# A memset of a scratch tile between GpSimd's row scatters in the 64-expert routing stages

## What is computed

```
x = x + 0.5 * _L0_ffn_ref(_layernorm(x), wg, shared_w1, shared_w2, expert_w1, expert_w2)
x = x + _L0_attn_ref(_layernorm(x), ...)
x = x + 0.5 * _L0_ffn_ref(_layernorm(x), ...)
...
```

## Time and profile before

| | us |
|---|---|
| median of 3 runs (3281.53 to 3283.92) | 3281.57 |
| span of the profiled execution | 3607.6 |
| TensorE busy in it | 2593.0 |
| VectorE busy | 2038.9 |
| GpSimd busy | 1846.4 |
| ScalarE busy | 1370.6 |
| scatters of line 1894, first routing stage, 160 | 159.7 |
| scatters of line 1894, second routing stage, 128 | 125.0 |

### The profile page before, as it was taken

How to read it: one execution, slowest core, us unless ns; L and a number is a source line. 1 busy time by engine, 2 the same in 40 slices (tenths; PEclk the granted TensorE clock), 3 DMA queues, 4 the chain that set the end, 5 groups by cost and what they waited for, 6 DMA issues and landing times. The chain is left out here.

```text
span 3607.6 us, 68811 instructions
## 1 busy us (share of the span) xinstructions
PE 2593.0 (72%) x24634; PEld 1681.5 (47%) x24634; DVE 2038.9 (57%) x5864; ACT 1370.6 (38%) x2937; POOL 1846.4 (51%) x2072
## 2 busy tenths in 40 slices
PE   1224994735499945689998899947388886999573
PEld 1113884423368834356555555536133332555362
DVE  4347334523443345547885587621699999787413
ACT  1111221301122222344665266622576763466323
POOL 5650775254317742126996213456488886123554
PEclk7666997856599977799999799978699999899786
DMA  9100896121019974331110101112221211111123
GB/s 373 48 1 8 213 224 155 45 66 31 27 41 226 226 191 108 138 120 21 19 19 3 20 19 30 48 55 56 102 94 48 94 62 40 22 20 35 43 80 92
DMA packets 222721, 294.13 MB, mean 82 GB/s; under 512 B 36704, under 2 KB 179583, under 8 KB 216288
## 3 DMA queue, kind: packets, MB, share of 16 engines
q1 hardware_dynamic: 172704, 249.85, 22.3%
q0 software_dynamic: 47616, 39.44, 5.8%
q10 hardware_dynamic: 2112, 1.05, 0.1%
HBM read 181.88 MB, written 107.12 MB: 80 GB/s over the span
## 5 line engine op out<-in xcount | busy, mean ns | idle before, releaser
L3783 POOL TENSOR_TENSOR l3am_db<-l3am_du,l3am_bs 128x1024 f32<-128x1024 f32 x127 | 298.0, 2367 | 39.9 <-DVE l3am_hh L4021 36.1
L4021 DVE TENSOR_TENSOR_SCAN l3am_hh<-l3am_dA,l3am_db 128x1024 f32<-128x1024 f32 x128 | 292.1, 2283 | 0.9 <-ACT l3am_dA L3921 0.7
L1217 POOL TENSOR_TENSOR l2a_pT<-l2a_pT,kept 128x512 int32<-128x512 int32 x213 | 265.1, 1280 | 45.4 <-ACT l2a_pT L1423 45.4
L3066 POOL DMA_INDIRECT l0f_table<-l0f2e_y,l0f2e_idx x128 | 178.9, 1398 | 177.1 <-DVE l0f2e_idx L3038 130.2
L3066 POOL DMA_INDIRECT l0f_table<-l0f1e_y,l0f1e_idx x128 | 179.6, 1403 | 139.2 <-DVE l0f1e_idx L3038 91.2
L4152 PE MATMUL l3am_y<-l3am_hc,ident 128*128 128x512 f32 x512 | 242.1, 596 | 0.0
L3921 ACT ACTIVATE l3am_dA<-l3am_dl,l3am_al 128x512 f32<-128x512 f32 x256 | 166.3, 682 | 130.8 <-DVE l3am_hh L4021 127.2
L1894 POOL DMA_INDIRECT l0f_rows<-l0f1r_row,l0f1r_idx x160 | 159.7, 998 | 103.1 <-issue 69.3
L1304 DVE CUSTOM_DVE_ANT_0 l2a_junk<-l2a_s,addend 128x256 f32<-128x256 f32 x486 | 178.1, 421 | 57.0 <-PE l2a_s L1540 44.6
L1297 DVE TENSOR_REDUCE l3f1a_mx<-l3f1a_s 128x2 f32<-128x512 f32 x243 | 156.5, 685 | 40.9 <-PE l3f1a_s L1540 32.4
L1297 DVE TENSOR_REDUCE l3f2a_mx<-l3f2a_s 128x2 f32<-128x512 f32 x243 | 156.4, 684 | 39.7 <-PE l3f2a_s L1540 32.1
(11 more groups left out here) (848 smaller groups left out, 7045.5 us busy)
## 6 DMA issues: line engine op xcount, KB each, us to landing
l3am_bs<-l3a_b SPq DMA_DIRECT2D x32, 1024.0 KB, 6.6
l0f1m_w<-in_L_ffn_expert_w SPq DMA_DIRECT2D x64, 384.0 KB
l0f2m_w<-in_L_ffn_expert_w SPq DMA_DIRECT2D x64, 384.0 KB
l1a_top<-l1a_kernel SPq DMA_DIRECT2D x16, 1024.0 KB, 12.6
l0f_rows<-blank SPq DMA_DIRECT2D x8, 1930.0 KB, 15.2
l0f1m_w<-in_L_ffn_expert_w SPq DMA_DIRECT2D x64, 192.0 KB
l0f2m_w<-in_L_ffn_expert_w SPq DMA_DIRECT2D x64, 192.0 KB
l3f_rows<-blank SPq DMA_DIRECT2D x8, 1440.0 KB, 11.6
```

What stands on the lines that cost most here:

```text
L1217: self.nc.gpsimd.tensor_tensor(t, t, self.kept[:, f // 8 % 2, :].unsqueeze(1).to_broadcast([P, 2, 2 * P]), ALU.mult).then_inc(self.cut_g, 1)
L3066: g.indirect_dma_start(out=tables[p], out_offset=bass.IndirectOffsetOnAxis(ap=idx[u % RING][:, a:a + 1], axis=0), in_=y[u % RING][:, a, :] ...
L3783: G.tensor_tensor(db[n % DB][:, :].rearrange("p (j t) -> p j t", j=CC), du[k % 2][:, :, :], bs[s // QUARTER][:, s % QUARTER, :].unsqueeze( ...
L4021: V.tensor_tensor_scan(hh[n % HH][:, :], dA[n % 2][:, :], db[n % DB][:, :], 0.0, ALU.mult, ALU.add).then_inc(h_ready, 1)
```

## The change

In `pool_scatter`, for the first three groups, GpSimd sets a tile of 128 x 384 numbers (`pause`) to zero before each scatter but the group's first. Each memset counts up a new semaphore (`paused`), and the next one waits for the count of the one before. That is 31 memsets per group, 93 per stage. The groups sent on a condition are left as they are. No other instruction reads the tile.

```diff
--- before.py
+++ after.py
@@ -1842,6 +1842,7 @@
     NONE = 65536.0
     SURE = -(-SLOTS // (K * GT))
     PER = 16 * TPG * K
+    PAUSE = 384
 
     def __init__(self, ph, c, m, front, logits, hidden, out, kept=GROUPS):
         E = self.E
@@ -1853,6 +1854,7 @@
         self.idx = [ph.sb(f"idx{i}", [P, TPG, self.K], U32) for i in range(self.DEPTH)]
         self.full = [ph.sb(f"full{i}", [P, 1], I32) for i in range(self.DEPTH)]
         self.least = ph.sb("leastf", [P, 1])
+        self.pause = ph.sb("pause", [P, self.PAUSE])
         self.base = ph.sb("base", [P, E])
         self.lg, self.gates, self.left, self.valid, self.key = (
             ph.sb(n, [P, TPG, E]) for n in ("lg", "gates", "left", "valid", "key"))
@@ -1874,6 +1876,7 @@
         self.h_done, self.silu_ready, self.gated, self.so_done, self.added = (
             ph.sem(s) for s in ("h_done", "silu_ready", "gated", "so_done", "added"))
         self.rows_free, self.sent = ph.sem("rows_free"), ph.sem("sent")
+        self.paused = ph.sem("paused")
         self.early = [ph.sem(f"early{i}") for i in range(2)]
         self.count = 0
 
@@ -1891,6 +1894,11 @@
         u = n % self.DEPTH
         for t in range(TPG):
             for j in range(self.K):
+                if (t or j) and n < self.SURE:
+                    k = n * (TPG * self.K - 1) + t * self.K + j - 1
+                    if k:
+                        g.wait_ge(self.paused, k)
+                    self.nc.gpsimd.memset(self.pause[:, :], 0.0).then_inc(self.paused, 1)
                 g.indirect_dma_start(out=self.m.rows, out_offset=bass.IndirectOffsetOnAxis(
                     ap=self.idx[u][:, t, j:j + 1], axis=0), in_=self.row[u][:, t, :], in_offset=None,
                     bounds_check=self.last_slot, oob_is_err=False).then_inc(sent, 16)
```

## The result

The changed kernel takes 3328.11 us (median of 4 runs, 3324.78 to 3330.27) against 3281.55 us before (3277.50 to 3283.92) in the same runs: a ratio of 1.014 with a 95% interval from 1.0125 to 1.0154, 46.6 us slower. The forecast was slower, 3348 us, in a range from 3283 to 3375.

What follows compares the result with a forecast made beforehand. The prediction took GpSimd's scatter sending to bound the first routing stage and nearly the second. 93 memsets per stage at 0.40 us cost 37 + 30 = 67 us on 3281.57, giving 3348 us, range 3283 to 3375.

Steps and rivals of the forecast that it cites:

- GpSimd's sending sets the stages' ends: Both routing stages: GpSimd's scatters end first stage by 9 us, fall 7 us short in second; 37 and 30 us paid.
- The memset's price: Each scatter with a memset: step 1.69 us against 1.28, so 0.40 us more, bounds 0.36 and 0.56.
- Memsets beside VectorE: Memsets writing while VectorE computes, both routing stages: bounded by nothing below and 8 us above, taken as nothing.
- Most of them exist only while every instruction and packet is recorded: Engine stalls while scatters are sent: said to come mostly with recording, their size matching the 326 us.
- The 326 us: Whole kernel: profiled span of 3607.6 us exceeds the plain median of 3281.57 us by 9.9%; charged to stalls under recording.
- The fall of the profiled span: Sign in the changed profile: span some 150 to 200 us shorter while plain runs get slower.
- The rebuilt undisturbed run: Plain run without stalls: first routing stage 108 us shorter than in the trace, second 169, later stages the other 49.
- Rival 1: Both routing stages: stalls are in plain runs too and pauses cure them, 194 us faster, 3088 us; chance 0.14.
- the prediction's cousin of rival 1: Behind scatters: late instruction blocks fetched by DMA stall plain runs too; 3088 us, little of rival 1's chance.

Runs made afterwards that it cites:

- e0: Kernel before, unchanged, profiled once more: 3279.94 us, ratio 1.0007, in a free batch (no engine held back).
- e1: Changed kernel with memsets in the first routing stage alone: 3312.01 us, ratio 1.0103 to the kernel before.
- e2: Changed kernel with memsets in the second routing stage alone: 3293.32 us, ratio 1.0047 to the kernel before.
- e3: Changed kernel with memsets of 128x16 instead of 128x384: 3280.64 us, ratio 1.0003 to the kernel before.
- e8: Changed kernel as it is, a second time: 3322.03 us against 3275.36 for the kernel before, ratio 1.0163.
- e4: Changed kernel with memsets of 128x192 instead of 128x384, held-back batch: 3513.94 us against 3607.50 for the kernel before, ratio 0.9719.
- e5: Changed kernel with memsets of 128x768 instead of 128x384, held-back batch: 3464.24 us against 3607.50 for the kernel before, ratio 0.9591.
- e7: Kernel before with the later groups' condition asked for each tile, 136 scatters for 160 in the first stage, held-back batch: 3584.12 us, ratio 0.9938.
- e9: Kernel before with later groups' condition asked per tile, plus memsets of 128x192 in the first stage, 128x384 in the second: 3298.43 us, ratio 1.0069.

## Why the prediction was right, and where it was not

**Slower because GpSimd's sending sets the stages' ends: shown.** e0's profile has GpSimd 20 us behind VectorE in the first stage (forecast 9) and 8 us ahead of it in the second (forecast 7). e1 makes the first stage 32 us longer with VectorE done at 235 us, e2 the second by 20 to 23, e3 neither.

**The memset's price: the term that was mis-sized.** The prediction took 0.98 + 0.13 + 0.42 + 0.16 = 1.69 us a step and 0.40 us a memset. The duration was 0.44 and the joint behind it 0.17, as taken, but the joint in front was 0.00 for 0.13: that row was a copy behind a scatter in another stage, and a memset starts at once. The price is 0.30 us, below the lower bound of 0.36. 93 x 0.30 = 28 us for 37 in each stage: 28 + 20 = 48 us for the 67 forecast, and 46.6 measured. This term makes 19 of the 20 us between 3348 and 3328.

**Memsets beside VectorE, bounded at 8 us and taken as nothing.** They lengthen VectorE's work by 14 us (2038.7 to 2052.9), 7 in each stage, more than the bound. That it cost nothing in the first stage is because GpSimd ends that stage by far: its end grew by 31 us, all of it GpSimd's sending. In the second stage what it may have cost is not told apart from the sending's 20 to 23 us.

**"Most of them exist only while every instruction and packet is recorded": the step that failed.** e0, e3 and e8 were recorded and have none of the stalls, and in the two held-back batches every timed run of the kernel before takes 3595 to 3638 us. The 326 us were the difference between a disturbed and an undisturbed batch, and I took the one variable that I could see, profiled or not, for the cause. The Trainium skill's page "NOTIFIC — the notification-queue block", section 7.1, was cited for a block that pushes back on its producers rather than lose a record. e0's trace bears out nothing of it for this kernel: as many instructions were recorded as in the first profile (68811), and no stall shows. The fall of the profiled span, named in advance as a sign (150 to 200 us, in fact 280), came, but from the batch.

**The rebuilt undisturbed run held all the same,** since it was worked out from rows and not from the cause. Forecast and e0: VectorE's side of the first stage 235 and 229 us, GpSimd's 244 and 252, what the stalls cost 108 and 100 us in the first stage, 169 and 165 in the second, 49 and 70 later. GpSimd's 8 us too few are mostly long scatters: e0's 160 took 163.8 us, 7 more than 160 x 0.98, and 12 of them over 1.2 us, of which the disturbed trace has 3. There was luck in it too: the runs of the result fell into a free batch, as the three before them had, and nothing in the prediction foresaw another kind.

**Rival 1 (the pauses cure the stalls, faster) is real where there are stalls.** Its mark, "1.28 us per scatter would be just too quick where 1.69 is not", holds for e4 in the first stage (1.43 us suffices) and for e5 in the second (1.90 us, not 1.43). It was priced against the wrong base: 194 us off 3281.57, where there is nothing to cure. From 3607 us it would be 3413. The widths beside the change's gave 3514 and 3464. Where a batch is held back the change's own result is open; its two neighbours in width make faster likely, and that is argued, not shown.

**What holds the engines back stays open.** The traces speak against some causes: the scatters take 0.98 us and start every 1.28 us in either condition; the 29 packets that fetched instructions in the second stage took 0.91 us on average in the first profile and 1.00 in e0, which speaks against late code, the prediction's cousin of rival 1; nor are there more packets (6144 of the scatters' queue in that stage in both). The granted clock is lower in held-back runs (0.85 to 0.86 on average, 0.88 to 0.89 in e0's), but where no rows are sent, in the 248 us behind the first stage, it is 0.96 in both profiles, and VectorE's busy time is the same (2038.9 and 2038.7 us); so the lower clock looks like a result of TensorE's idle time, which no run tests. What the chip's other cores did during a batch is in no record. Even spacing against mean rate, and e3's narrow memsets in a held-back batch, were not run.

## What to carry to other kernels

When a profiled execution is several per cent off the timed runs, profile the same kernel again before giving the gap a cause: one profile can't tell recording from a condition of the machine. An instruction that goes into an engine's idle time costs only what it and its joint exceed of that time, and the joint has to be read from the same pair of kinds. A pause that lets held-back engines go pays only while they are held back; in the other condition its price is paid on whatever engine sets the end, so measure both before keeping it. A memset on GpSimd also lengthens instructions of VectorE beside it, so look at that engine's busy time before a longer one is taken.

## What was not expected of the hardware

- The same kernel has two times 10% apart, 3275 to 3282 and 3607 to 3618 us, stable within 1% through a batch, and one chip showed both in turn (e4 to e7, then e8 and e9).
- In the slower condition the engines are held back while indirect scatters are issued every 1.28 us, and the memset from which they run depends on the stage: 128x192, a step of 1.43 us, frees the first stage (VectorE busy 36.5 of 47 us), not the second (6.9 of 45), which 128x768, a step of 1.90 us, frees (45.7 of 59).
- Some of VectorE's instructions take longer beside a memset of GpSimd: a TENSOR_SCALAR of 128x128 took 1.50 us (median) beside a memset of 128x768, 0.35 without; a TENSOR_TENSOR of 128x1024 took 1.22 us in either case (e5).
- Behind a scatter GpSimd has 0.30 us in which a memset of 128x16 is free; 128x192, 128x384 and 128x768 took 0.28, 0.44 and 0.76 us and made the step 1.43, 1.58 and 1.90 us.
- A value loaded from SBUF into a register of GpSimd, with its checks, took 0.55 us (e9), and nine that weren't needed cost 5 us on the path.
